# A graph layer with edge groups of 1024 instead of 512, and its linear attention moved into the edge loop

## The chip, the cores and the metric

One core of a Trainium2 chip. The metric is the device time of one execution in microseconds (us). A profiled execution has a span of its own, from its first to its last recorded instruction; the execution's device time is a little longer. The engines are PE (TensorE, matrix products), DVE (VectorE), ACT (ScalarE), POOL (GpSimd) and SP (SyncE, which here only issues DMAs).

## The reference

The input is `x`, 3125 nodes of 256 features, and 50,000 edges sorted by their target node. In short:

```python
xn = layernorm(x)                                   # without scale and shift
h  = einsum('ni,hio->hno', xn, W)                   # 4 heads of 64
e  = leaky(attn_src[:, src] + attn_dst[:, dst], 0.2) * edge_weight
e_exp = exp(e - max(e))                             # one maximum over all edges and heads
alpha = e_exp / (segment_sum(e_exp, dst)[dst] + 1e-10)
gnn = segment_sum(h[:, src] * alpha, dst)
q, k, v = split(xn @ W_qkv)                         # 4 heads of 32
k = softmax(k over the nodes); context = k^T v; mix = (context, q * 32**-0.5) @ W_out + b_out
x1 = x + gnn + mix
n2 = layernorm(x1); weights = n2 @ wr + br
y  = (gelu(n2 @ w1 + b1) @ w2 + b2) * weights       # for the 1561 nodes of highest weight, else 0
out = x1 + y + n2
```

All products are in fp32. The division by the sum of the exponentials is made once per node at the end, so the edge work only accumulates `h[src] * e_exp` and `e_exp` per target node.

## The kernel before, in words

Nodes are held in 25 blocks of 128 (`NB`), in groups of `BODY` = 5. `x`, the accumulator `acc` (260 columns: 256 features and 4 denominators) and most else stay in SBUF. The kernel has three stages.

**First stage.** DVE normalises a block (`normed`, L742), PE turns it (two transposes, L429), ACT copies it to `xnT` (L603). PE's `project` then multiplies it with a weight of 392 columns (L414: `h`, the two attention terms of the edges, and `v`; two contraction halves, and each fp32 product is recorded as two passes, so 4 passes) and makes `k` and `q` (L420, 8 passes of 128 columns), which ACT copies out (L592). DVE's `evacuate_h` copies the 260 columns `h` and `attn_src` to `hst` (L749) and the other 132 to `adv` (L750). SP stores each block's `hst` to the table `htab` in DRAM (`store_rows`, L282). Between those stores SP also issues the loads of late weights and, from block 15 to 22, the index lists of edge groups 0 to 7 (`step`, L293 to L300, five DMAs per group). POOL adds `b_out` to `x` block by block (L362).

**Edge stage.** Edges are taken in groups of `TILES` x 128 = 512, 98 groups. For each, POOL issues 4 indirect DMAs, each gathering 128 rows of `htab` by source node into `G` (L380). `G` has `RING` = 4 groups, the lists `LISTS` = 8. POOL waits for the list and, from group 4 on, until DVE has read the old group out of the slot (`messages_ready`). The work per group g:

- DVE builds `ohT`, the edges' columns of one target block (L855); PE's `expand` multiplies it with `attn_dst` (L449, 12 small products); DVE adds the gathered `attn_src` (L896), takes the leaky part and the edge weight (L900, L904) and the maximum (L908, `rm`).
- PE's `turn` lays the 128 maxima along a row (L470), DVE's `group_max` (L915) makes the running maximum, ACT takes the exponentials (L656 into `msg`, L657 into PSUM), DVE multiplies the gathered rows with them (`messages`, L921) and builds the one-hot matrix `oh` of the targets within their block (L983).
- PE's `sums` multiplies `oh` with `msg` (L474, 4 tiles, 8 passes of 260 columns), and DVE's `add_last` adds the result to `acc` of the block, scaled by the change of the maximum (L926). ACT computes that scale (`rescale`, L633, L636). A group that lies across two node blocks (24 of the groups) has its sums split by ACT with two masks (`split_sums`, L646) and added twice by DVE.

`et`, `msg`, `oh` and the PSUM banks of `sums` exist twice. DVE makes the logits of group g+2 and the columns of g+3 while group g is summed, and adds the sums of g-1 during step g. On every engine the edge loop is written by `groups` (L204): 8 steps unrolled, a hardware loop of 11 turns with 8 steps each, and 10 steps unrolled.

**Linear attention.** It stands between the preparation of the first edge groups and the edge loop: ACT exponentiates `k` (L611); PE turns each block of it (L508) and sums `v` against it (L512); the context is multiplied by `W_out` into `C2` (L517, L1015); PE multiplies each block's `q` by `C2` (L522, 2 passes of 256 columns) and DVE adds it to `x` (L1019). Only then DVE and PE enter the edge loop.

**Tail.** DVE divides and adds (L1062, L1066), normalises again, PE runs the two products of the feed-forward part (L552, L565), DVE ranks the weights by counting (L1111, L1114), POOL weights the result, SP stores it.

Each engine runs its own program in order; the order is written out by hand, and semaphores join the engines.

Of the kernel before, what the change touches and what calls it, by code (L numbers as in the profile page):

```python
# [19 lines left out]
TILES = 4  # L20
RING = 4
LISTS = 8
BODY = 5


def gps_layer(nc, x_in, src_in, dst_in, ew_in, gw_in, gas_in, gad_in, wqkv_in, wout_in, bout_in,
# [25 lines left out]
    ADV = HEADS + QK  # L52
    HW = ROW + ADV
# [8 lines left out]
    LOOPS = NG // LISTS  # L62
    KSEL = max(1, int(0.5 * N))
    KK = KSEL - 1 if KSEL > 1 else 1
    assert EREST % TILES == 0 and D == HF == 256 and NB % BODY == 0 and QK == P

    htab = nc.dram_tensor("htab", (NB * P, ROW), F32, kind="Internal").ap()
    dstu_d = nc.dram_tensor("dstu_d", (NG, GE), U16, kind="Internal").ap()
    dstm_d = nc.dram_tensor("dstm_d", (NG * GE,), I32, kind="Internal").ap()
    meta_d = nc.dram_tensor("meta_d", (NG, 3), I32, kind="Internal").ap()  # L70
    low_d = nc.dram_tensor("low_d", (NG, 1), I32, kind="Internal").ap()
    w_d = nc.dram_tensor("w_d", (NB, P), F32, kind="Internal").ap()

    with ExitStack() as ctx:
# [10 lines left out]
        kq = sb("kq", [P, 2, NB * P])  # L85
        adv = sb("adv", [P, NB, ADV])
        wbig = sb("wbig", [P, KC, HW])
        wqk = sb("wqk", [P, KC, 2 * QK])
# [8 lines left out]
        boutb = sb("boutb", [P, D])  # L97
# [7 lines left out]
        xnT = sb("xnT", [P, BODY, KC, P])  # L105
# [15 lines left out]
        meta = sb("meta", [1, NG * 3], I32)  # L121
        neg1 = sb("neg1", [1, PAD], I32)
# [5 lines left out]
        dmr = sb("dmr", [P, LISTS, TILES], I32)  # L128
# [10 lines left out]
        et = sb("et", [P, 2, 17])  # L139
        rm = sb("rm", [P, 2])  # L140
# [9 lines left out]
        kmaxs = sb("kmaxs", [P, NB // BODY])  # L150
        ekt = sb("ekt", [P, BODY, P])
# [6 lines left out]
        dm = wide[0:NG, 0:GE].bitcast(I32)  # L158
# [6 lines left out]
        wrow = kq[:, 0, :]  # L165
        junk = kq[:, 1, :]
# [6 lines left out]
        for name in ("constants_ready y_weighted gelu_table masks_ready k_padding_zero wqkv_loaded "  # L173
                     "block_iota_ready kmax_of_batch sp_go gp_go dve_go act_go deviation_ready b_out_loaded "
                     "w_loaded late_weights_loaded a_loaded w_times_a w_a_ready stats_ready mean_var_ready "
                     "rstd_ready xn_ready xn_turned xnT_ready h_projected rows_staged attn_dst_v_taken "
                     "kq_projected kq_taken b_out_added dst_loaded table_steps tables_stored ranges_loaded "
                     "last_dst_loaded padding_loaded attn_dst_split kmax_steps k_exp ksum_steps ek_turned "
                     "ek_taken context_summed context_taken c2_multiplied c2_taken mix_multiplied mix_added "
# [17 lines left out]
        FIRST_BATCHES = ((0, 1), (1, BODY - 1))  # L197
        TURN_BANKS, MIX_BANKS = (3, 4, 6), (3, 4, 6)
        WT_AT = 6
        DLP = 12  # L200

        block = ctx.enter_context(nc.Block())

# [947 lines left out]
```

## Time and profile before

| | us |
|---|---|
| three executions | 818.95, 821.65, 824.38 |
| median | 821.65 |
| profiled execution, device time | 820.17 |
| its span | 818.0 |
| busy: PE, DVE, POOL, ACT | 666.8, 593.3, 467.2, 224.4 |
| mean granted TensorE clock (1 is full speed) | 0.849 |

The busy time of PE counts modelled ends of pipelined products. The shares over the whole span mix the three stages, so the stages have to be read one by one. The page also lists where the chain of work that ended last went: PE 28%, issue 21%, DVE 17%, POOL 14%, DMA 11% ("issue" is time in which an engine waited for nothing that the profile shows).

### The profile page before, as it was taken

Reading aid. Unit: us, or ns where it says so; the run is one execution under the profiler, and the core shown is the slowest. Engines: PE = TensorE matmul, PEld = TensorE weight load, DVE = VectorE, ACT = ScalarE, POOL = GpSimd, SP = SyncE. Lnnn points to the kernel's source line nnn. Section 1 sums busy time; section 2 is a strip of 40 time slices with the busy share of each in tenths; the row PEclk is TensorE's granted clock in tenths of the full one; section 3 lists DMA queues with packets and bytes.
Section 4 is the critical chain, followed back from the end, with each engine's and each line's share of the span. In section 5 each row is a group of like instructions: output and inputs, shape, how many; then the busy total and the mean of one; then the engine's idle time right before and its main releaser. Section 6 shows DMA issues by size and latency. Waiting matters only on the chain.

```text
span 818.0 us, 18313 instructions
## 1 busy us (share of the span) xinstructions
PE 666.8 (82%) x4271; PEld 548.8 (67%) x4272; DVE 593.3 (73%) x1631; ACT 224.4 (27%) x817; POOL 467.2 (57%) x512
## 2 busy tenths in 40 slices
PE   3799687776878786878886878788859989999995
PEld 2577575554656564756675666666648879999994
DVE  7566268666767685867686868687789973989895
ACT  1132512111222122213232323232333423323331
POOL 5134246777777777777777777777721350333332
PEclk9899888887787678778677978686888989999998
DMA  7264325655556565656555555566410001000000
GB/s 212 58 181 75 87 72 114 138 138 136 134 135 143 131 139 134 140 133 138 137 135 134 139 135 138 132 138 140 108 35 1 1 12 71 33 26 27 27 27 22
DMA packets 104859, 82.97 MB, mean 101 GB/s; under 512 B 67133, under 2 KB 91566, under 8 KB 104561
## 3 DMA queue, kind: packets, MB, share of 16 engines
q0 software_dynamic: 18816, 52.21, 24.9%
q1 hardware_dynamic: 85873, 29.16, 16.8%
q14 instruction: 145, 1.19, 0.5%
q8 instruction: 25, 0.41, 0.2%
HBM read 74.47 MB, written 6.84 MB: 99 GB/s over the span
## 4 chain that ended last, share of the span: by engine, by line
PE 28%; issue 21%; DVE 17%; POOL 14%; DMA 11%; DVEq 5%; SPq 2%; ACT 1%; ACTq 0%; POOLq 0%
POOL G L380 13%; DMA G<-htab,srcr 9%; PE ps L552 8%; PE ps L565 8%; PE ps L414 4%; PE ps L474 4%; DVE msg L921 3%; PE ps L420 2%; DVEq L228 2%; DVE wprod L1079 1%; DMA x<-in_x 1%; DVE oh L983 1%; DVE G L1062 1%; DVE x L1066 1%; DVE x L1019 1%
## 5 line engine op out<-in xcount | busy, mean ns | idle before, releaser
L380 POOL DMA_INDIRECT G<-htab,srcr x392 | 372.9, 951 | 150.7 <-issue 127.7
L474 PE MATMUL ps<-msg,oh 128*128 128x260 f32 x784 | 265.9, 498 | 78.4 <-DVE oh L983 76.8
L474 PEld LDWEIGHTS ps<-msg,oh 128*128 128x128 f32 x784 | 183.0, 245 | 116.2 <-issue 83.3
L921 DVE TENSOR_TENSOR msg<-G,ps 128x1024 f32<-128x1024 f32 x98 | 118.7, 1212 | 29.1 <-issue 28.1
L552 PEld LDWEIGHTS ps<-xnT,w 128*128 128x128 f32 x800 | 98.3, 201 | 3.8 <-issue 1.8
L552 PE MATMUL ps<-xnT,w 128*128 128x128 f32 x800 | 98.8, 285 | 2.1 <-ACT wide L712 1.6
L656 ACT ACTIVATE msg<-et,negR 128x16 f32<-128x16 f32 x98 | 30.1, 308 | 224.2 <-DVE rj L915 178.7
L565 PE MATMUL ps<-w,wide 128*128 128x256 f32 x400 | 90.4, 380 | 1.0 <-DVE acc L1086 1.0
L565 PEld LDWEIGHTS ps<-w,wide 128*128 128x128 f32 x400 | 74.3, 190 | 10.2 <-issue 1.3
L393 POOL TENSOR_SCALAR G<-acc,mw 128x256 f32<-128x256 f32 x25 | 23.1, 923 | 99.6 <-DVE mw L1119 90.4
L983 DVE TENSOR_TENSOR oh<-ps,dmr 128x512 f32<-128x512 f32 x98 | 67.2, 686 | 17.0 <-issue 16.8
L449 PE MATMUL ps<-ad,ohT 128*128 x1464 | 77.3, 176 | 2.4 <-DVE ohT L855 1.3
L470 PEld LDWEIGHTS ps<-ident,rm 128*128 128x128 f32 x196 | 43.2, 243 | 49.9 <-DVE rm L908 43.1
L449 PEld LDWEIGHTS ps<-ad,ohT 128*128 128x128 bf16 x1464 | 67.3, 118 | 8.5 <-issue 2.5
L470 PE MATMUL ps<-ident,rm 128*128 128x128 f32 x196 | 51.4, 352 | 22.4 <-DVE rm L908 22.2
L712 ACT ACTIVATE wide<-ps,b 128x128 f32<-128x128 f32 x200 | 54.3, 390 | 3.5 <-PE ps L552 3.4
L386 POOL TENSOR_TENSOR x<-x,acc 128x256 f32<-128x256 f32 x25 | 22.0, 885 | 48.7 <-DVE acc L1072 48.7
L1114 DVE TENSOR_SCALAR_CACHE_REDUCE kq<-kq,wtok 128x3125 f32<-128x3125 f32 (+24 forms) x25 | 46.6, 1865 | 0.0
L633 ACT ACTIVATE fsc<-negRlast,negR 128x1 f32 x98 | 28.8, 294 | 61.4 <-issue 30.1
L1111 DVE TENSOR_SCALAR_CACHE_REDUCE kq<-kq,wtok 128x128 f32<-128x128 f32 (+23 forms) x24 | 44.9, 1871 | 0.0
L414 PE MATMUL ps<-wbig,xnT 128*128 128x392 f32 x100 | 40.5, 531 | 4.9 <-DVE adv L750 4.7
L855 DVE TENSOR_SCALAR ohT<-dstb,nodeid 128x512 bf16<-128x512 uint16 x98 | 38.0, 387 | 8.5 <-issue 7.2
(135 smaller groups left out, 722.5 us busy)
## 6 DMA issues: line engine op xcount, KB each, us to landing
dstb<-dstu_d SPq DMA_DIRECT2D x98, 128.0 KB
G<-htab,srcr POOLq DMA_INDIRECT x392
htab<-hst SPq DMA_DIRECT2D x25, 130.0 KB, 2.8
out<-G SPq DMA_DIRECT2D x24, 128.0 KB, 1.7
x<-in_x SPq DMA_DIRECT2D x4, 640.0 KB, 8.0
w<-in_L_ffn_w SPq DMA_DIRECT2D x4, 512.0 KB
kq<-w_d SPq DMA_DIRECT2D x1, 1600.0 KB, 6.4
dmr<-dstm_d SPq DMA_DIRECT2D x98, 2.0 KB
```

The lines of the kernel that those rows point to most:

```text
L380: gp.indirect_dma_start(G[:, q % RING, k, :], None, htab, bass.IndirectOffsetOnAxis(ap=srcr[:, q, k:k + 1], axis=0)).then_inc(s_g[q % RING ...
L414: m = pe.matmul(ps[:, 2 + b, 0:HW], xnT[:, t % BODY, kc, :], wbig[:, kc, :], start=(kc == 0), stop=(kc == KC - 1))
L449: m = pe.matmul(ps[:, p, 4 * k:4 * k + 4], ohT[:, columns, k:GE:TILES], ad3[:, bass.ds(b, 1), j, :].rearrange("p a h -> p (a h)"), start=F ...
L470: pe.matmul(ps[:, 2, 0:P], rm[:, q % 2:q % 2 + 1].to_broadcast([P, P]), ident[:, :], start=True, stop=True).then_inc(S["max_turned"], 1)
L474: m = pe.matmul(ps[:, 3 + p, 0:ROW], oh[:, p, k, :], msg[:, p, k, :], start=(k == 0), stop=(k == TILES - 1))
L552: m = pe.matmul(ps[:, 2 + half, (c % 4) * P:(c % 4 + 1) * P], w1[:, kc, c * P:(c + 1) * P], xnT[:, t % BODY, kc, :], start=(kc == 0), stop ...
L565: m = pe.matmul(ps[:, 4 + t % 3, 0:D], hT[:, t % 2, c, :], w2[:, c, :], start=(c == 0), stop=(c == FC - 1))
L712: m = act.activation(hT[:, t % 2, c, :], ps[:, 2 + half, (c % 4) * P:(c % 4 + 1) * P], ACT.Gelu_apprx_tanh, bias=b1[:, c:c + 1])
L921: dve.tensor_tensor(msg[:, p, :, 0:HF].rearrange("p k (h o) -> p k h o", h=HEADS), G[:, q % RING, :, 0:HF].rearrange("p k (h o) -> p k h o ...
L983: dve.tensor_tensor(oh[:, q % 2, :, :], iotap.unsqueeze(1).to_broadcast([P, TILES, P]), dmr[:, q, :].unsqueeze(2).to_broadcast([P, TILES, ...
L1111: dve.tensor_scalar(junk[:, 0:lo], wrow[:, 0:lo], wt, 0.0, ALU.is_ge, ALU.add, accum_out=cnt[:, t, 0:1]).then_inc(S["counted"], 1)
L1114: dve.tensor_scalar(junk[:, lo:N], wrow[:, lo:N], wt, 0.0, ALU.is_gt, ALU.add, accum_out=cnt[:, t, 1:2]).then_inc(S["counted"], 1)
```

## The change

- **First stage.** `wbig` has 264 columns (`h` and both attention terms), so `project` is 4 passes of 264 columns and nothing else. `xnT` keeps all 25 blocks. `evacuate_h` moves from DVE to ACT (260 columns to `hst`, 4 to `adst`). `k` is projected after the last block, in 7 chunks of 512 nodes (`keys`), which DVE takes together with their maximum. The tables of the edges (`table_steps`) lose two steps on DVE and one cast moves to ACT. `b_out` is no longer added to `x` by POOL, which zeroes `acc` block by block instead. Blocks 1 to 9 of `x` are loaded by ACT's queue. Of the lists SP issues only that of group 0 before the last stores (at block 19); the other three and the late weights come behind them.
- **Edge stage.** Groups of 1024 (`TILES` = 8), 49 of them, `RING` = 2, `LISTS` = 4, four list DMAs per group. Messages, one-hot matrices and sums go in two halves of 4 tiles; POOL waits for the first half of the messages before the first 4 gathers and for the second half before the other 4. `et`, `rm`, `msg`, `oh` and the bank of `sums` exist once. DVE makes the logits of group g+1 in step g, all four operations in a row, and adds the sums of g at the end of step g itself. `dmod`, the target within its block, is masked by DVE instead of loaded. PE's program is written out for all 49 groups; the other engines loop over turns of 4 groups.
- **Linear attention.** It runs inside the loop: during groups 3 to 22 PE makes `v` of one block and the turned `k` (`make_pair`), ACT copies both out (`take_pairs`); at group 23 the context is closed and multiplied into `M` = (W_q x `C2`), so that the second half multiplies `xnT` itself by `M` (`mix`, with `b_out` as a first product with a row of ones, 6 passes of 256 columns) and DVE adds the result to `x` (`add_mix`). One block per group, two in every fourth (`BLOCKS`).
- **Tail.** Unchanged.

The core of the diff ("-" before, "+" after):

```diff
-TILES = 4
-RING = 4
-LISTS = 8
+TILES = 8
+HALF = 4
+RING = 2
+LISTS = 4
+BLOCKS = ((0,), (1,), (2,), (3, 4))
...
-        xnT = sb("xnT", [P, BODY, KC, P])
+        xnT = sb("xnT", [P, NB, KC, P])
-        msg = sb("msg", [P, 2, TILES, ROW])
-        oh = sb("oh", [P, 2, TILES, P])
+        msg = sb("msg", [P, TILES, ROW])
+        oh = sb("oh", [P, TILES, P])
...
# SP
                 for t in range(NB):
                     store_rows(t)
-                    if 2 <= t < 2 + len(loads):
-                        sp.dma_start(loads[t - 2][0], loads[t - 2][1])...
-                    if NB - LISTS - 2 <= t < NB - 2:
-                        step(t - (NB - LISTS - 2), t - (NB - LISTS - 2))
-                groups(step, peeled=False)(sp)
+                    if t == TABLES_AT:            # 9
+                        store_tables()
+                    if t == TABLES_AT + 6:
+                        spread_tables()
+                    if t in LISTS_AT:             # (19,)
+                        step(LISTS_AT.index(t), LISTS_AT.index(t))
+                unrolled(step, range(len(LISTS_AT), LISTS))
+                for tile, array in loads:
+                    sp.dma_start(tile, array).then_inc(S["late_weights_loaded"], 16)
+                looped(sp, 1, LOOPS - 1, step)
+                unrolled(step, TAIL)
...
# POOL
+                for k in range(TILES):
+                    if k % HALF == 0 and (g is None or g >= RING):
+                        gp.wait_ge(S["messages_ready" if k else "messages_half"], n)
+                        gp.sem_inc(S["gp_go"], 1)
+                    gp.indirect_dma_start(G[:, q % RING, k, :], None, htab, ...)
...
# PE
+            def sums(g):
+                ...
+                pe.wait_ge(S["added_last"], g + 1)
+                pe.wait_ge(S["messages_half"], g + 1)
+                pe.wait_ge(S["onehot_half"], g + 1)
+                add_messages(range(HALF))
+                pe.wait_ge(S["messages_ready"], g + 1)
+                pe.wait_ge(S["onehot_last"], g + 1)
+                add_messages(range(HALF, TILES)).then_inc(S["summed_last"], 1)
+            def mix(t):
+                bank = 4 + t % BODY % 2
+                if t:
+                    pe.wait_ge(S["mix_added"], t + 1 if t % BODY in (0, 1, 2, 3) else t)
+                pe.matmul(ps[:, bank, 0:D], ones[:, :], bout[:, :], start=True, stop=False)
+                for kc in range(KC):
+                    m = pe.matmul(ps[:, bank, 0:D], xnT[:, t, kc, :], M[:, kc, :], start=False, stop=(kc == KC - 1))
+                m.then_inc(S["mix_multiplied"], 1)
+            for g in range(NG):
+                sums(g)
+                if g + 1 < NG:
+                    turn(g + 1)
+                if g + 2 < NG:
+                    if g % 2 == 0:
+                        load_ranges(pe, regs, cursor, (g + 2) % LISTS)
+                    expand(g + 2)
+                if MADE_AT <= g < MADE_AT + TURNS * LISTS:      # 3 to 22
+                    ... make_pair(i * BODY + s)
+                if g == MIXED_AT:                               # 23
+                    multiply_context()
+                if MIXED_AT <= g < MIXED_AT + TURNS * LISTS:    # 23 to 42
+                    ... mix(i * BODY + s)
...
# ACT
+            def evacuate_h(t):
+                act.wait_ge(S["h_projected"], t + 1)
+                if t >= BODY:
+                    act.wait_ge(s_tab[t % BODY], 16 * (t // BODY))
+                act.activation(hst[:, t % BODY, :], ps[:, 2 + t % 2, 0:ROW], ACT.Copy)...
+                act.activation(adst[:, t, :], ps[:, 2 + t % 2, ROW:HW], ACT.Copy)...
...
+                rescale(fsc, p, last, "factor_last", n, "max_kept_last")
+                if side:
+                    side(q)
+                split_sums(q)
...
# DVE
+            def step(g, q, side=None):
+                dve.wait_ge(S["exp_ready"], n)
+                visit(g, q)            # messages, one-hot, messages, one-hot
+                if g is None or g + 1 < NG:
+                    if g is None or g + 1 < NG - 1:
+                        mask_dst((q + 1) % LISTS)
+                    logits((q + 1) % LISTS, n1, g if g is None else g + 1)
                 if g is None or g + 2 < NG:
+                    if q % 2 == 0:
+                        load_ranges(dve, regs, cursor, (q + 2) % LISTS)
+                    columns((q + 2) % LISTS)
+                if g is None or g + 1 < NG:
+                    group_max(q + 1, n1)
+                if side:
+                    side(q)
+                add_last(q)
...
-            groups(step)(dve)
+            unrolled(step, FIRST)
+            looped(dve, 1, 1 + TURNS, step)
+            take_context()
+            looped(dve, 1 + TURNS, LOOPS - 1, step, add_mix)
+            unrolled(step, TAIL)
```

## Rows read from the trace of the kernel before

**Rows 1.** Windows by stage: length; PE, PEld, DVE, ACT, POOL busy; clock, DMA share, GB/s.

```profile
126.00:300.00 174.00, 137.75 (x849) 106.03 (x847) 121.65 (x359) 38.00 (x155) 131.83 (x139) 0.79 0.61 136
...
608.50:818.00 209.50, 187.94 (x1251) 176.22 (x1251) 170.18 (x407) 67.71 (x234) 63.29 (x75) 0.95 0.07 24
```

**Rows 2.** Groups of instructions, by line: busy us, mean ns, idle before and its releasers.

```profile
L380 POOL DMA_INDIRECT G<-htab,srcr x392 | 372.9, 951 | 150.7 <-issue 127.7 <-DVE msg L921 23.0
L474 PE MATMUL ps<-msg,oh 128*128 128x260 f32 x784 | 265.9, 498 | 78.4 <-DVE oh L983 76.8 <-issue 1.4
```

**Rows 3.** Timeline of POOL: start us, us, engine, line, operation, [idle before <-releaser].

```profile
94.40 1.16 POOL L380 DMA_INDIRECT G<-htab,srcr  x1 [20.41 <-issue]
...
125.73 0.94 POOL L380 DMA_INDIRECT G<-htab,srcr  x1 [11.43 <-DVE msg L921]
...
306.46 0.95 POOL L380 DMA_INDIRECT G<-htab,srcr  x1 [0.30 <-DVE msg L921]
...
596.56 0.95 POOL L380 DMA_INDIRECT G<-htab,srcr  x1 [0.30 <-issue]
```

**Rows 4.** Timeline of the first stage.

```profile
26.06 0.40 DVE L742 TENSOR_SCALAR xn<-x,mv,rstd 128x256 f32<-128x256 f32 x1
...
77.78 0.38 PE L429 MATMUL ps<-ident,xn 128*128 128x128 f32 x2
78.00 1.48 PE L414 MATMUL ps<-wbig,xnT 128*128 128x392 f32 x4
...
80.43 1.48 PE L414 MATMUL ps<-wbig,xnT 128*128 128x392 f32 x4
...
84.16 0.43 DVE L749 COPY hst<-ps 128x260 f32<-128x260 f32 x1 [1.58 <-PE ps L414]
...
90.52 0.82 SPq L282 DMA_DIRECT2D htab<-hst  x2
```

**Rows 5.** Chain that ended last: start us, us, what.

```profile
90.91 2.27 DMA htab<-hst
```

**Rows 6.** Groups by line: copies on ACT and the attention's add on DVE.

```profile
L636 ACT ACTIVATE negRlast<-negR 128x1 f32 x122 | 24.8, 203 | 14.4
L603 ACT ACTIVATE xnT<-ps 128x256 f32<-128x256 f32 x25 | 9.4, 376 | 2.2 <-PE ps L429 2.2
L1019 DVE TENSOR_TENSOR x<-ps,x 128x256 f32<-128x256 f32 x25 | 10.6, 425 | 2.6 <-PE ps L522 2.4
```

**Rows 7.** Timeline of the last groups.

```profile
598.34 0.57 PE L449 MATMUL ps<-ad,ohT 128*128 x12
...
599.57 0.17 DVE L896 TENSOR_TENSOR et<-ps,G 128x16 f32<-128x16 f32 x1
...
600.94 0.49 PE L470 MATMUL ps<-ident,rm 128*128 128x128 f32 x2 [0.17 <-DVE rm L908]
...
602.71 0.34 DVE L915 TENSOR_SCALAR_CACHE_REDUCE rj<-ps,negR 128x128 f32<-128x128 f32 x1
...
603.60 1.22 DVE L921 TENSOR_TENSOR msg<-G,ps 128x1024 f32<-128x1024 f32 x1
604.74 0.68 DVE L983 TENSOR_TENSOR oh<-ps,dmr 128x512 f32<-128x512 f32 x1
605.16 0.88 ACT L646 ACTIVATE hst<-ps,mask 128x260 f32<-128x260 f32 x2 [1.59 <-PE ps L474]
...
605.57 1.99 PE L474 MATMUL ps<-msg,oh 128*128 128x260 f32 x8 [0.63 <-DVE oh L983]
...
606.99 0.49 DVE L926 SCALAR_TENSOR_TENSOR acc<-acc,fsc,hst 128x260 f32 x1 [0.24 <-DVE acc L926]
...
608.03 0.48 DVE L926 SCALAR_TENSOR_TENSOR acc<-acc,fsc,ps 128x260 f32 x1 [0.55 <-PE ps L474]
```

**Rows 8.** Timeline at a loop jump.

```profile
322.54 1.22 DVE L921 TENSOR_TENSOR msg<-G,ps 128x1024 f32<-128x1024 f32 x1 [3.19 <-issue]
...
324.50 3.81 PE L474 MATMUL ps<-msg,oh 128*128 128x260 f32 x8 [3.80 <-DVE oh L983]
```

More of the change, by code:

```diff
@@ L72, in gps_layer @@
     w_d = nc.dram_tensor("w_d", (NB, P), F32, kind="Internal").ap()
+    NORMED = ((0, 1), (1, BODY - 1)) + tuple((lo, BODY) for lo in range(BODY, NB, BODY))
     with ExitStack() as ctx:
@@ new lines, in sums @@
+                pe.wait_ge(S["messages_half"], g + 1)
[4 more added lines that the diff above has]
+                add_messages(range(HALF, TILES)).then_inc(S["summed_last"], 1)
+            load_ranges(pe, regs, cursor, 0)
+            expand(0)
+            expand(1)
+            for c in range(2, CHUNKS):
+                keys(c)
+            pe.wait_ge(S["k_taken"], CHUNKS)
@@ new lines, in _, with add_context @@
+            for kc in range(KC):
+                m = pe.transpose(ps[:, 5, kc * P:(kc + 1) * P], wqkv[:, kc, 0:QK], ident[:, :])
+            m.then_inc(S["query_turned"], 1)
+            pe.matmul(ps[:, 6, 0:P], zrow[:, 0:P], zrow[:, 0:P], start=True, stop=False, skip_group_check=True)
+            turn(0)
+            def add_context(t):
+                pe.wait_ge(S["pair_taken"], t + 2)
+                return pe.matmul(ps[:, 6, 0:P], pair[:, t % BODY, 0:P], pair[:, t % BODY, P:2 * P], start=False, stop=(t == NB - 1), skip_group_check=True)
@@ new lines, in make_pair @@
+            def make_pair(t):
+                bank = 4 + t % BODY % 2
+                if t == 0:
+                    pe.wait_ge(S["query_taken"], 1)
+                    pe.wait_ge(S["k_padding_zero"], 1)
+                pe.wait_ge(S["k_exp"], 1 + t // BODY)
+                if t:
+                    pe.wait_ge(S["pair_taken"], t + 1 if t % BODY in (0, 1, 2, 3) else t)
+                for kc in range(KC):
+                    pe.matmul(ps[:, bank, 0:P], xnT[:, t, kc, :], wqkv[:, kc, 2 * QK:3 * QK], start=(kc == 0), stop=(kc == KC - 1))
+                pe.transpose(ps[:, bank, P:2 * P], kT[:, t * P:(t + 1) * P], ident[:, :]).then_inc(S["pair_made"], 1)
+                if t >= 2:
+                    add_context(t - 2)
@@ new lines, in _ @@
+            load_ranges(dve, regs, cursor, 0)
+            columns(0)
+            dve.wait_ge(S["attn_dst_last"], 1)
+            columns(1)
+            for c in range(CHUNKS):
+                lo, hi = c * WIDE, min((c + 1) * WIDE, N)
+                dve.wait_ge(S["k_projected"], c + 1)
+                dve.tensor_scalar(kT[:, lo:hi], ps[:, 5 + c % 2, 0:hi - lo], 1.0, LOWEST, ALU.mult, ALU.max, accum_out=kmaxs[:, c:c + 1]).then_inc(S["k_taken"], 1)
+            dve.memset(kT[:, N:NB * P], 0.0).then_inc(S["k_padding_zero"], 1)
@@ new lines, in add_mix @@
+            def add_mix(q):
+                for s in BLOCKS[q]:
+                    t = dve.snap(u, min_val=0, max_val=NB - 1)
+                    a = x[:, bass.ds(t, 1), :].rearrange("p a c -> p (a c)")
+                    dve.wait_ge(S["mix_multiplied"], mixed)
+                    dve.sem_inc(S["dve_go"], 1)
+                    dve.tensor_tensor(a, ps[:, 4 + s % 2, 0:D], a, ALU.add).then_inc(S["mix_added"], 1)
+                    dve.reg_add(u, u, 1)
+                    dve.reg_add(mixed, mixed, 1)
```

669 lines of the change are left out of this document (293 added, 376 removed).

## The prediction

> **What bounds the kernel now.** I read the windows by stage first [rows 1]. The edge stage runs at a mean granted clock of .79 of the full level, with POOL at 131.8 of 174 us and neither PE nor DVE full; the tail takes 209.5 us and the diff does not touch it. Next, the groups of instructions: 392 gathers of .951 us each, and almost all of POOL's idle time before them is "issue" [rows 2]. POOL's timeline then gives the skeleton of the run [rows 3]: the first gather starts at 94.40, one stall of 11.43 us stands at 125.73 (DVE and PE are in the linear attention and do not free the ring), the last gather ends at 597.51. (597.51 - 94.40 - 11.13) / 392 = 1.255 us per gather, and a gather with its usual gap is .95 + .30 = 1.25. So POOL issues without pause, and everything else keeps up. The span is first gather 94.4 + gathers 492.0 + stall 11.1 + drain to the last add 11.0 (608.51 - 597.51) [rows 3, 7] + tail 209.5 = 818.0; the profiled execution took 820.17, so 2.2 us lie around the span. It stands .2% under the median 821.65.
>
> Two further things bear on the change. The first gather waits for the table's last store, issued from 90.52 although its rows were staged at 84.16: SP was issuing lists in between [rows 4]. It lands 2.27 us after 90.91 [rows 5], and POOL starts 1.2 us later. And the loop is not as smooth as POOL shows it: at a jump DVE loses 3.19 us of "issue" and the sums after it run in 3.81 us instead of 1.99 [rows 7, 8], the two levels of the clock (1.2 and 2.4 GHz). The ring of four groups absorbs this; POOL's own jump costs it .30, no more than any gap [rows 3].
>
> **First stage: a certain gain.** A block now costs 2.43 us (78.00 to 80.43) [rows 4]. PE keeps .22 for the turning (77.78 to 78.00) and 4 passes of 264 columns; the sums' passes of 260 columns take 1.99 / 8 = .25 each [rows 7], so 1.0, and with an estimated .06 between them 1.28 us per block. ACT beside it copies xnT .38, 260 columns .44 (half of .88) and 4 columns .20 [rows 6, 7]: 1.02, hidden, but only .26 short of becoming the bound. DVE no longer evacuates, so block 5, the first that waits for PE, is normalised about 1.7 us before its 26.06 [rows 4], at 24.4. Twenty blocks at 1.28 are 25.6; I add 2.5 for a start at half clock (two blocks twice as long) and 1.2 for the last block's turning: 53.7. Then .45 for the copy, .39 to the issued store (90.52 to 90.91), 2.27 and 1.2: **first gather at 58.0**, bounds 54 (no slow start, block 0 earlier) and 63 (1.5 us per block). SP issues one list before the last stores and 12 list DMAs behind them, .41 each [rows 4], 5 us, before the second group's gathers end. The 25 small memsets that replace the 25 adds on POOL lie before its first gather, beside the projections.
>
> **Gathers: unchanged.** 392 x 1.255 = 492.0. The fifth list DMA per group and the attention's own stall (11.1) go; what keeps POOL waiting now is counted as X below.
>
> **The loop: what is paid for the gain.** POOL needs 8 x 1.255 = 10.04 us per group of 1024. With single buffers the rest becomes one serial chain per group, read off the last groups [rows 7]: messages to sums 1.97 (603.60 to 605.57), the sums s, about .1, turn .49, about .05, maximum to messages .89 (602.71 to 603.60): 3.5 + s. The expansion (24 products, 2 x .57) and the logits lie beside the sums. For 16 passes s is 3.98 at the full level, 7.62 at half [rows 7, 8], and by the mean of all groups 2 x 265.9 / 98 = 5.43 [rows 2]. The chain is then 7.5, 11.1, or 8.9: under POOL's 10.04 by 1.1 on the mean, over it at half clock, and the ring now holds two groups. I take the mean, since the work per edge on PE is nearly the same, and keep the other two as ends.
>
> What comes on top in the second half: add_mix .43 [rows 6] before add_last, which itself moves into the chain: .48 after the sums, less cover, +.35 in an ordinary group; in one that lies across two blocks the split .88 and the second add .73 (.24 + .49) [rows 7], +1.1; I take .88, as 14 of the groups 24 to 43 are such. Two blocks fall into every fourth group, +.43. DVE's jump, now every four groups, costs about 2.9 (3.19 less its .30), and the sums behind it run at half clock, +2.2 against the mean. Four groups: 4 x (8.93 + .88) + .43 + 2.9 + 2.2 = 44.8 against POOL's 40.2: 4.6 lost, five times, 23. In the first half the pair's passes lie in PE's gaps and the split comes less often: 4 x 9.4 + 2.9 = 40.5 with no dip, some .6 lost, five times, 3. Start-up: the second group's successor waits for the exponentials of the keys in front of group 0's; between 0 and the 11.4 of before's stall [rows 3] I take 2, because only seven chunks and five exponentials are left there. Closing the context at group 23 is a serial chain of about ten short steps over DVE, PE and ACT at .4 to .5 each [rows 6, 7]: 5, bounds 2 and 8. The last groups all lie across blocks: 7. **X = 40**, ends 9 (chain always 7.5 + extras, under POOL) and about 72 (mean s between mean and half clock). Unrolling PE in itself I cost at nothing: at the jump PE waits for DVE's one-hot, not for itself [rows 8].
>
> **Drain.** From the last gather to the first logits 2.06 (597.51 to 599.57), to the turn's end 1.9, then maximum to messages 1.2, messages to sums 2.0, 16 passes 4.0 to 7.6, split and two adds 2.1 [rows 7]: 13 to 17 with POOL last, up to 19.5 if the chain runs behind POOL, as I expect there; I take 17.5.
>
> **Sum:** 58.0 + 492.0 + 40 + 17.5 + 209.5 = 817.0, plus 2.2 around it: **819 us**, 1 less than the profiled run, .3% under the median. Break-even is X = 42.
>
> At this point the Trainium skill speaks against the change: "Double-buffer for performance: Overlap DMA with compute" (Trainium Kernel Development and Optimization, Best Practices), where the change halves each buffer's number. By it alone rival B would be the forecast; the mean chain of 8.9 under 10.04 says that one buffer still suffices between jumps.
>
> **Rivals.** *A, the clock stays up.* If the passes of the attention keep PE at the full level in the loop, s = 3.98, the chain 7.5 to 8.8 absorbs the jumps, X = 9, drain 14: 58 + 492 + 9 + 14 + 209.5 + 2.2 = 785. For: PE's work is spread evenly; the tail, dense, shows .95 [rows 1]. Against: .79 in the loop with the attention outside it, and a chain with more serial waits than before. *B, the serial chain (slower).* If s is 6.5, midway between mean and half, the chain is 10.0 and always lags: first half 4 x 10.5 + 2.9 = 44.9, 4.7 lost five times; second half 4 x 10.88 + .43 + 2.9 = 46.9, 6.7 lost five times; with 2 + 5 + 8 for the rest X = 72, drain 19.5: **853**. For: every wait in the chain lets PE idle, and the sums after an idle stretch are the slow ones [rows 8]. Against: the mean of before includes such waits. It decides from X = 51 on. *C, the jump gets cheaper.* DVE's loop body has four steps instead of eight, and POOL's short body shows no jump cost at all [rows 3]. Then the jump costs .30 and its dip goes: X = 14, 793. The Trainium skill has a rule that could make this so (Runtime: NRT & Kernel Launch, Instruction fetch mechanics): a taken branch to a target outside the resident instructions waits for a fetch. Against: four steps of 1024 in halves hold nearly as many instructions as six of the old. *D, the first stage does not do what it promises:* ACT and its waits for the stores pace it, 2.0 per block, first gather at 72: 833.
>
> **How the numbers follow.** Forecast (X from 27 to 54: 806 to 834) .46; A .22 (776 to 794); B .18 (840 to 866); C .08; D .06. A change of 1% is 8.2 us: about what can be told from no change here. Faster (under 813.4): A, C and .12 of the forecast's range, .42. Slower (over 829.9): B, .07 of the forecast and .05 of D, .30. The rest, .28, lies within 1%. Cases of both signs hold most of it; the likeliest one's own range is 806 to 834. The range 778 to 858 takes in most of A and B and leaves out about .1 of each side's tails together.
>
> **What will show it.** First gather at 58 (54 to 63): later means ACT or the late lists, seen as what ends PE's idle time before the projection. POOL's idle time "<-DVE msg", 23.0 before, should grow to about 40 and sit mostly at the jumps of the second half; none there is A or C (told apart by the sums' mean, 5.4 against 4.0 per 16 passes, and by DVE's "issue" at the jump), in every group is B. The granted clock in the loop near .79. From the last gather to the last add 17.5. The tail 209.5; another length would make the forecast wrong by a mechanism that I have not seen.

## The result

The changed kernel takes 813.41 us (median of 11 executions, 810.47 to 815.19) against 819.48 us before (median of 11, 816.63 to 824.38): ratio .9917, 95% interval .99 to .9934. That is .8% faster, inside the band of 1% that the prediction called no change, and 5.6 us under the 819 that it gave. The profiled execution took 810.47 with a span of 808.7, so it is the lowest of the eleven; a stage read from it is a few us better than the median.

### The profile page after: what moved, and what is told of

The parts are those of the page before. It is cut to its first block, busy times and chain, and to the rows that moved or that the text cites. A ratio compares the mean times of both kernels' runs of the same rounds, so it can differ in the third digit from the quotient of the medians.

```text
span 808.7 us, 15213 instructions
## 1 busy us (share of the span) xinstructions
PE 700.1 (87%) x4447; PEld 594.0 (73%) x4448; DVE 518.4 (64%) x1246; ACT 185.9 (23%) x651; POOL 452.5 (56%) x511
## 4 chain that ended last, share of the span: by engine, by line
PE 50%; POOL 15%; issue 14%; DVE 14%; DMA 4%; DVEq 2%; ACT 1%; ACTq 0%; POOLq 0%; SPq 0%
PE ps L489 15%; POOL G L387 14%; PE ps L600 8%; PE ps L613 8%; PE ps L465 7%; PE ps L561 3%; DMA G<-htab,srcr 3%; PE ps L424 2%; PE ps L559 2%; DVE wprod L1110 1%; DVE stats L794 1%; DVE G L1093 1%; PE ps L437 1%; DVE x L1097 1%; DVE msg L937 1%
## 5 line engine op out<-in xcount | busy, mean ns | idle before, releaser
L387 POOL DMA_INDIRECT G<-htab,srcr x392 | 373.9, 954 | 162.0 <-issue 124.6
L489 PE MATMUL ps<-msg,oh 128*128 128x260 f32 x784 | 246.3, 483 | 28.8 <-DVE oh L951 28.6
L465 PE MATMUL ps<-ad,ohT 128*128 x1752 | 116.5, 201 | 13.1 <-DVE ohT L908 9.4
L465 PEld LDWEIGHTS ps<-ad,ohT 128*128 128x128 bf16 x1752 | 112.3, 167 | 16.0 <-issue 15.0
L951 DVE TENSOR_TENSOR oh<-ps,dmod 128x512 f32<-128x512 f32 x96 | 65.5, 682 | 0.0
L699 ACT ACTIVATE hst<-ps,mask 128x260 f32<-128x260 f32 x48 | 20.3, 473 | 169.8 <-PE ps L489 169.8
L932 DVE TENSOR_SCALAR_CACHE_REDUCE rj<-ps,negR 128x128 f32<-128x128 f32 x48 | 16.7, 348 | 47.5 <-PE ps L485 45.1
L1145 DVE TENSOR_SCALAR_CACHE_REDUCE xnT<-kT,wtok 128x3125 f32<-128x3125 f32 (+24 forms) x25 | 46.6, 1865 | 0.0
L1142 DVE TENSOR_SCALAR_CACHE_REDUCE xnT<-kT,wtok 128x128 f32<-128x128 f32 (+23 forms) x24 | 44.9, 1870 | 0.0
L908 DVE TENSOR_SCALAR ohT<-dstb,nodeid 128x1024 bf16<-128x1024 uint16 x49 | 24.3, 496 | 31.4 <-issue 28.8
L561 PE MATMUL ps<-M,xnT 128*128 128x256 f32 x100 | 37.3, 508 | 0.0
```

The lines of the kernel that those rows point to most:

```text
L387: gp.indirect_dma_start(G[:, q % RING, k, :], None, htab, bass.IndirectOffsetOnAxis(ap=srcr[:, q, k:k + 1], axis=0)).then_inc(s_g[q % RING ...
L465: m = pe.matmul(ps[:, p, 4 * k:4 * k + 4], ohT[:, columns, k:GE:TILES], ad3[:, bass.ds(b, 1), j, :].rearrange("p a h -> p (a h)"), start=F ...
L489: m = pe.matmul(ps[:, 3, 0:ROW], oh[:, k, :], msg[:, k, :], start=(k == 0), stop=(k == TILES - 1))
L561: m = pe.matmul(ps[:, bank, 0:D], xnT[:, t, kc, :], M[:, kc, :], start=False, stop=(kc == KC - 1))
L908: dve.tensor_scalar(ohT[:, 0, :], dstb[:, q, :], nodeid[:, bass.ds(last, 1)], None, ALU.is_equal).then_inc(S["columns_last"], 1)
L951: return dve.tensor_tensor(oh[:, tiles, :], iotap.unsqueeze(1).to_broadcast([P, HALF, P]), d.unsqueeze(2).to_broadcast([P, HALF, P]), ALU. ...
```

## The profile after, beside the one before

The windows by stage of the changed kernel, the columns as in [rows 1]:

```profile
110.00:207.00 97.00, 80.79 (x512) 68.49 (x511) 56.04 (x128) 14.68 (x52) 71.77 (x77) 0.83 0.52 135
...
318.00:450.00 132.00, 126.44 (x780) 101.04 (x778) 77.37 (x185) 21.89 (x79) 89.68 (x95) 0.81 0.47 121
...
583.00:599.00 16.00, 11.82 (x35) 9.07 (x34) 6.94 (x14) 2.34 (x8) 0.00 (x0) 0.68 0.03 8
599.00:808.70 209.70, 187.39 (x1252) 175.52 (x1251) 171.12 (x408) 69.08 (x238) 63.25 (x75) 0.94 0.07 24
```

The first number after the length is PE's busy time. In the first half of the loop it is 80.8 of 97 us; in the second half 126.4 of 132, that is 96%, where the kernel before had 137.8 of 174 (79%) [rows 1]. The clock is no lower than before (.83 and .81 against .79). So PE has become full, which the prediction had looked for nowhere.

The groups of instructions (busy us, mean ns, idle before and its releasers):

```profile
L387 POOL DMA_INDIRECT G<-htab,srcr x392 | 373.9, 954 | 162.0 <-issue 124.6 <-DVE msg L937 37.4
L489 PE MATMUL ps<-msg,oh 128*128 128x260 f32 x784 | 246.3, 483 | 28.8 <-DVE oh L951 28.6
L465 PE MATMUL ps<-ad,ohT 128*128 x1752 | 116.5, 201 | 13.1 <-DVE ohT L908 9.4 <-DVE ohT L905 3.7
L561 PE MATMUL ps<-M,xnT 128*128 128x256 f32 x100 | 37.3, 508 | 0.0
L559 PE MATMUL ps<-bout,ones 1*128 1x256 f32 x50 | 20.8, 499 | 0.7 <-ACT M L744 0.7
```

The sums take 246.3 / 49 = 5.03 us per group of 1024 (5.43 by the rows of before), and PE waits for VectorE's one-hot only 28.6 us in all against 76.8 [rows 2]. New are 58 us of mix (L561, L559).

POOL's timeline, which answers to [rows 3]; the rows with a wait of over 2 us before them, and the first and the last gather:

```profile
57.78 1.16 POOL L387 DMA_INDIRECT G<-htab,srcr  x1 [10.70 <-issue]
...
82.94 0.94 POOL L387 DMA_INDIRECT G<-htab,srcr  x1 [5.27 <-DVE msg L937]
...
206.53 0.96 POOL L387 DMA_INDIRECT G<-htab,srcr  x1 [2.38 <-issue]
...
332.44 0.94 POOL L387 DMA_INDIRECT G<-htab,srcr  x1 [6.86 <-DVE msg L937]
...
356.04 0.94 POOL L387 DMA_INDIRECT G<-htab,srcr  x1 [2.35 <-issue]
...
420.32 0.94 POOL L387 DMA_INDIRECT G<-htab,srcr  x1 [4.57 <-DVE msg L937]
...
505.75 0.94 POOL L387 DMA_INDIRECT G<-htab,srcr  x1 [4.54 <-DVE msg L937]
...
508.93 0.94 POOL L387 DMA_INDIRECT G<-htab,srcr  x1 [2.23 <-issue]
...
551.09 0.94 POOL L387 DMA_INDIRECT G<-htab,srcr  x1 [3.51 <-DVE msg L937]
...
582.03 0.95 POOL L387 DMA_INDIRECT G<-htab,srcr  x1 [0.30 <-issue]
```

These rows give the balance, with the numbers of before from [rows 3, 7]. The first gather is 36.6 us earlier (94.40 to 57.78) and the attention's stall of 11.1 is gone: 47.7 gained. Given back: POOL waits 32.1 us between the gathers (each wait of over .45 less its usual .30), 1.1 in smaller ones, and the drain from the last gather to the last add grew from 11.0 to 18.4 (582.98 to 601.39). The tail is 2.2 shorter. -47.7 + 32.1 + 1.1 + 7.4 - 2.2 = -9.3, the difference of the spans (818.0 - 808.7).

The 32.1 us by place: 5.0 at group 2, 6.6 at group 26 (the closing of the context), 9.9 in the groups 30 to 42, of them 4.3 at group 34 and 4.2 at group 42, 4.6 in the groups 46 to 48, and 6.1 in three pauses of POOL that name no releaser ("issue", groups 14, 28 and 42). POOL's group 34 goes into the slot of group 32 and waits for the messages of that group. What lies behind this wait is seen in PE's and VectorE's timeline some groups earlier, where group 31 ends and VectorE's loop jumps to group 32:

```profile
401.83 2.97 PE L465 MATMUL ps<-ad,ohT 128*128 x47
404.74 0.69 PE L559 MATMUL ps<-bout,ones 1*128 1x256 f32 x2
405.36 1.13 PE L561 MATMUL ps<-M,xnT 128*128 128x256 f32 x4
406.42 1.12 PE L559 MATMUL ps<-bout,ones 1*128 1x256 f32 x2
407.47 2.08 PE L561 MATMUL ps<-M,xnT 128*128 128x256 f32 x4
409.34 5.67 PE L489 MATMUL ps<-msg,oh 128*128 128x260 f32 x16
414.85 0.39 PE L485 MATMUL ps<-ident,rm 128*128 128x128 f32 x2
...
408.23 0.19 DVE L926 TENSOR_REDUCE rm<-et 128x1 f32<-128x32 f32 x1
...
415.27 0.35 DVE L932 TENSOR_SCALAR_CACHE_REDUCE rj<-ps,negR 128x128 f32<-128x128 f32 x1 [5.89 <-PE ps L485]
...
418.31 1.22 DVE L937 TENSOR_TENSOR msg<-G,ps 128x1024 f32<-128x1024 f32 x1 [0.23 <-issue]
```

PE has no gap at all here: the expansion of a group that lies across two blocks (2.97), two blocks of mix (404.74 to 409.34, the second at half clock), then the sums. The maximum of the next group was ready at 408.42 and is turned at 414.85, because the sums stand before it. VectorE waits 5.89 us for it. And the jump itself, at 418.31, costs .23 us of "issue", where before it cost 3.19 [rows 8].

## Experiments

Ratios are to the kernel before, measured beside each run; the changed kernel has .9917, from the runs of the section on the result. A profile shows one execution, and the one shown can lie some us off the median. Theory P was formed from the rows above: PE's own work is the bound of the second half, and the wait falls where two blocks of mix stand between two sums. Its rival J is the prediction's term (VectorE's jump and a serial chain of single buffers). Theory S concerns the start: the first gather is not what counts there.

### VectorE's loop written out

```diff
-            looped(dve, 1, 1 + TURNS, step)
+            for g in range(TURNS * LISTS):
+                step(None, g % LISTS)
             take_context()
-            looped(dve, 1 + TURNS, LOOPS - 1, step, add_mix)
+            for g in range(TURNS * LISTS):
+                step(None, g % LISTS, add_mix)
```

> The changed kernel with VectorE's two loops of the edge stage written out (40 steps, the same instructions in the same order), so that VectorE never jumps between groups. Theory P (TensorE's own work is the bound of the second half: 126.4 us busy of 132 us between 318 and 450 in the changed kernel, and the waits of GpSimd lie where two blocks' products stand between two sums): no change, 813 +- 3 us, and the waits of 4.3 to 4.6 us at the groups 34 and 42 stay. Rival J (the prediction's term: VectorE's jump costs about 2.9 us every four groups and the sums behind it run at half clock): the waits at 34 and 42 go, 10 to 20 us less, 793 to 803 us.

Measured: 814.63 us, ratio .9919 (.9893 to .9945), no change. POOL's timeline has the same waits:

```profile
423.51 0.94 POOL L387 DMA_INDIRECT G<-htab,srcr  x1 [3.99 <-DVE msg L937]
...
508.88 0.94 POOL L387 DMA_INDIRECT G<-htab,srcr  x1 [4.17 <-DVE msg L937]
```

The jump costs nothing; J's price for it is refuted.

### b_out added by GpSimd

```diff
+                gp.tensor_tensor(x[:, t, :], x[:, t, :], boutb[:, :], ALU.add)...
...
-                pe.matmul(ps[:, bank, 0:D], ones[:, :], bout[:, :], start=True, stop=False)
```

> The changed kernel without the product of a row of ones and b_out in each block's mix (4 passes instead of 6); GpSimd adds b_out to x in the first stage, as the kernel before did, where it is idle. Theory P: a third of the mix leaves TensorE (20.8 us busy in all); between the groups 24 and 48 GpSimd waits 14 us outside its own 2 us pauses, of which about 9 hang on the mix; 5 to 9 us less, 804 to 808 us. Rival J: VectorE's order and jumps are the same, within 2 us of 813.

Measured: 803.04 us, ratio .9765 (.9733 to .9797), 1.5% or 12 us less than the changed kernel; more than expected. POOL's waits in the groups 27 to 45 (without its own pauses) fall from 9.9 to .5, those of the last three from 4.6 to 3.7, all waits from 32.1 to 24.8. The two profiled executions differ by 6.3 us (804.15 against 810.47), less than the medians, because the changed kernel's is its best one and this one lies 1 us over its median. PE is now at 117 of 132 us:

```profile
318.00:450.00 132.00, 117.35 (x764) 97.27 (x763) 80.36 (x191) 22.27 (x80) 92.17 (x98) 0.81 0.47 124
```

A third of the mix off PE is enough to free POOL in the groups 27 to 45. P holds.

### One block of the mix per group

```diff
-                if MIXED_AT <= g < MIXED_AT + TURNS * LISTS:
-                    i, s = divmod(g - MIXED_AT, LISTS)
-                    for s in BLOCKS[s]:
-                        mix(i * BODY + s)
+                if MIXED_AT <= g < MIXED_AT + NB:
+                    mix(g - MIXED_AT)
```

(and VectorE's adds alike, in its last five steps too)

> The changed kernel with the 25 blocks of the mix spread over the groups 24 to 48, one each, instead of over 24 to 43 with two in every fourth. Same products and adds in all. Theory P: the waits of 4.3 us at group 34 and 4.2 at group 42 shrink to under 1 each, the last five groups get one mix each more (about 2.5 us of TensorE at half clock, of which they have little to spare: up to 5 us given back); 2 to 8 us less, 805 to 811 us. Rival J: nothing moves at the jumps, the waits at 34 and 42 stay, 813 or a few us more.

Measured: 799.66 us, ratio .9745 (.9712 to .9777), 1.7% or 14 us less; more than expected, and the five later blocks cost nothing: the waits of the last three groups went from 4.6 to 1.6. At the two places POOL's rows are now:

```profile
418.62 0.95 POOL L387 DMA_INDIRECT G<-htab,srcr  x1 [0.76 <-DVE msg L935]
...
501.02 0.95 POOL L387 DMA_INDIRECT G<-htab,srcr  x1 [0.74 <-DVE msg L935]
```

The same work, laid otherwise, takes 14 us less with PE nearly as full in this stretch (124.6 of 132), so how the load lies is what hurt, more than its sum. The edit changes two things in that: no group has two blocks any more, and a fifth of the mix moves out of the groups 24 to 43 into the last five. The two are not told apart. The size of the ring is no part of it: `G` holds 16 tiles of 128 rows in both kernels (4 x 4 and 2 x 8), and the kernel before carried the 3.2 us of a jump with them [rows 8].

### The keys' exponentials behind the first groups

```diff
-            for i in range(NB // BODY):
-                exponentiate(i)
...
+            for g in FIRST:
+                step(g, g)
+                exponentiate(g)
+            exponentiate(LISTS)
```

> The changed kernel with the five exponentials of the keys on ScalarE moved from before the first group's exponentials to behind the steps of groups 0 to 3. Theory S (the 5.0 us wait of GpSimd at group 2 is set by the chain keys, exponentials of the keys, exponentials of group 0, messages, and not by the gathers): the wait goes and nothing later takes it back, 4 to 5 us less, 808 to 809 us. Rival G (given back): the second half, where TensorE is full, starts earlier but ends no earlier, 812 to 814 us.

Measured: 810.99 us, ratio .9873 (.9848 to .9898), .4% or 4 us less (the intervals just do not meet). That lies between S and G. The wait at group 2 is halved, not gone: 2.67 at 81.33 instead of 5.27. What is left is the keys' own products, the first half of them at half clock (granted .50 from 63.5 to 69), and a table load of 1.28 us that now stands in front of the first group's exponentials. The rows of the changed kernel show the whole chain:

```profile
63.51 10.04 PE L437 MATMUL ps<-xnT,wqkv 128*128 128x512 f32 x20
...
74.96 1.28 ACT L674 ACT_TABLE_LOAD   x1
76.26 0.83 ACT L674 ACTIVATE kT<-kT,kmax 128x640 f32<-128x640 f32 x1
...
80.27 0.30 ACT L716 ACTIVATE msg<-et,negR 128x32 f32<-128x32 f32 x1
```

### The expansion in one product of 12 columns

```diff
-                    for j in range(3):
-                        m = pe.matmul(ps[:, p, 4 * k:4 * k + 4], ..., ad3[:, bass.ds(b, 1), j, :]...)
+                    m = pe.matmul(ps[:, p, 12 * k:12 * k + 12], ..., ad3[:, bass.ds(b, 1), :, :]...)
...
+                dve.tensor_reduce(ekh, ps[...].rearrange("p (k j h) -> p k h j", ...), AX.X, ALU.add)...
```

> The changed kernel with the three parts of attn_dst in one product of 12 columns instead of three of 4 (584 products in the expansion instead of 1752), VectorE sums the three parts in one more operation of about .25 us per group. Theory P: TensorE's expansion falls from 116.5 us to about 40 and its load below GpSimd's 10.04 us per group; the waits at the groups 34, 42 and 46 to 48 shrink to a few tenths, the drain after the last gather by about 1; 8 to 13 us less than the changed kernel, ratio to the kernel before .976 to .982. Rival C (clock): with less work TensorE is granted the half level for longer, and the operation on VectorE lengthens the chain; ratio .988 to 1.00.

Measured: 800.02 us, ratio .977 (.9741 to .9798), 1.5% less: P, with its number. The three parts were three loads of the same one-hot weights. The mean of one product is the same with three times the columns, and since the products overlap, PE is busy 75 ns per product (43.9 / 584) where it was 66 (116.5 / 1752):

```profile
L464 PE MATMUL ps<-ad,ohT 128*128 x584 | 43.9, 206 | 15.1 <-DVE ohT L907 9.2 <-DVE ohT L904 5.9
```

The waits of the last three groups are gone, the drain is 16.8 instead of 18.4. The wait at group 42 stays at 3.6: the two blocks in the fourth group are still there. The clock between 318 and 450 stays at .81, against rival C.

### The kernel before, with its lists late

```diff
-                    if NB - LISTS - 2 <= t < NB - 2:
-                        step(t - (NB - LISTS - 2), t - (NB - LISTS - 2))
+                    if t == 15:
+                        step(0, 0)
+                for q in range(1, LISTS):
+                    step(q, q)
```

> The kernel before with one thing of the changed one: the index lists of the groups 1 to 7 are issued behind the table's last stores instead of between them (group 0's at block 15). The first gather should start near 88.5 instead of 94.4. Theory S (the start of the gathers is not the start that counts: group 2's ring slot, or in this kernel the linear attention's end, sets when GpSimd goes on): the wait of 11.43 us at 125.7 grows by what the start gains, no change, 820 +- 2. Rival G (the prediction counted this as 6 us of the gain): 5 to 6 us less.

Measured: 816.35 us, ratio .9961 (.9946 to .9976), 3 us less. The rows:

```profile
86.41 1.16 POOL L382 DMA_INDIRECT G<-htab,srcr  x1 [13.80 <-issue]
...
120.55 0.94 POOL L382 DMA_INDIRECT G<-htab,srcr  x1 [14.11 <-DVE msg L923]
```

The start is 8.0 earlier, the wait 2.7 longer. Neither S (nothing) nor G (5 to 6) is right: the stall is set by the attention's end, as S says, but that end came 5.2 us earlier too (125.73 to 120.55). The trace of the kernel before shows what waited. VectorE takes the first groups' logits before it goes on with the attention, and there it waited for the gathered rows, 6.66 us and 2.84 us; with the early gathers its first such wait is .93 (at 94.13).

```profile
101.17 0.17 DVE L896 TENSOR_TENSOR et<-ps,G 128x16 f32<-128x16 f32 x1 [6.66 <-DMA G<-htab,srcr]
...
106.18 0.17 DVE L896 TENSOR_TENSOR et<-ps,G 128x16 f32<-128x16 f32 x1 [2.84 <-DMA G<-htab,srcr]
```

### All four lists before the last store

```diff
-        TABLES_AT, LISTS_AT = 9, (19,)
+        TABLES_AT, LISTS_AT = 9, (20, 21, 22, 23)
```

> The changed kernel with all four first lists issued by SP before the table's last store (at the blocks 20 to 23) instead of one. The first gather should start about 4 us later, near 62. Theory S (the wait of 5.3 us at group 2 is set by the keys' chain, so the first gather has as much to spare): the wait at group 2 shrinks by what the start loses, same time within 2 us. Rival G (the start counts in full, as the prediction summed it): 4 us more, ratio .996 to .998.

Measured: 817.35 us, ratio .9963 (.9945 to .998), .5% or 4 us more than the changed kernel. The first gather is not 4 but 8.2 us later, at 66.01, and the wait at group 2 is gone:

```profile
66.01 1.16 POOL L387 DMA_INDIRECT G<-htab,srcr  x1 [18.25 <-issue]
```

So the wait at group 2 is set by the keys, as S says, and the time still rises, as G says. By the medians, 8.2 later less 5.0 absorbed leaves 3.2, near the 4 measured. The traces do not show this sum: POOL's waits from group 26 on (without its own pauses) are 24.7 instead of 21.0, and its last gather ends 8.0 later (590.96 against 582.98), so most of what was saved at group 2 is waited again later. The changed kernel's trace is its fastest execution and this one is near its median. How much later the first gather may start for nothing stays open.

### GpSimd's loop written out

```diff
-            looped(gp, 1, LOOPS - 1, step)
+            for g in range((LOOPS - 2) * LISTS):
+                step(None, g % LISTS)
```

> The changed kernel with GpSimd's loop of the edge stage written out. GpSimd pauses 2 to 4 us with no releaser at the second gather of the groups 14, 28 and 42 in every profile of the changed kernel and its variants, 112 gathers apart, and nowhere in the kernel before. If its instruction stream is the cause (fetch at the loop), the three pauses go or move; if it is something that counts gathers (a ring of descriptors), they stay at the same gathers. Time in the first case up to 6 us less, in the second the same within 2 us.

Measured: 812.49 us, ratio .9922 (.9893 to .9951), no change, and the three pauses stand at the same gathers:

```profile
207.81 0.95 POOL L387 DMA_INDIRECT G<-htab,srcr  x1 [3.62 <-issue]
...
355.74 0.94 POOL L387 DMA_INDIRECT G<-htab,srcr  x1 [2.36 <-issue]
...
508.65 0.94 POOL L387 DMA_INDIRECT G<-htab,srcr  x1 [2.23 <-issue]
```

So POOL's loop is not the cause: the pauses go with the number of the gather. That number alone isn't the cause either, for the kernel before makes the same 392 gathers without a pause. What it is stays open.

### Without the mix

The second half of the attention is left out, products and adds.

```diff
-                if MIXED_AT <= g < MIXED_AT + TURNS * LISTS:
-                    ...
-                        mix(i * BODY + s)
...
-            looped(dve, 1 + TURNS, LOOPS - 1, step, add_mix)
+            looped(dve, 1 + TURNS, LOOPS - 1, step)
```

> The changed kernel without the second half of the attention: the products of mix and their adds are left out (x gets neither context nor b_out); all else stays. Theory P: the waits at the groups 30 to 42 go; those at 26, 46 to 48 and the three pauses stay, about 21 of 32 us: 9 to 14 us less than the changed kernel, ratio .975 to .981, no better than e3, which keeps the whole work. Rival (the chain of single buffers itself lags): some 4 us less, ratio .987.

Measured: 799.40 us, ratio .9756 (.9729 to .9784), as P expected, and no better than the even mix (.9745), which does all the work. POOL's waits add up to the 21 us of the expectation, but not at its places: those of the last three groups are gone too, and 2.8 are left in the groups 27 to 45. One thing was not expected, in the windows of this kernel:

```profile
318.00:450.00 132.00, 107.57 (x698) 88.85 (x698) 75.59 (x179) 22.10 (x79) 91.92 (x97) 0.76 0.47 124
```

With 18.9 us less work on PE the granted clock is .76 instead of .81, and the sums take 260.8 us instead of 246.3. So part of what the mix costs PE, it gives back to the sums. This is the one run that shows it: with a third of the mix away, or with the expansion merged, the clock of the same stretch stays at .81, and with all four edits it is .83, though PE has less work there in each of them (117.4, 111.9 and 95.9 us).

### Three and four of the edits together, and an earlier first group

> The edits of e2, e3 and e4 together, with the three products per tile kept. Theory P: with one mix of 4 passes per group TensorE stays just under GpSimd in the second half, but the drain and the last groups keep the long expansions: 3 to 6 us behind the kernel with all four, ratio .965 to .973. Rival: the expansion is what counts, ratio .974 or more.

Measured: 796.71 us, ratio .9734 (.9695 to .9774), at the edge of the range given, with an interval that takes in P's range and its rival's, so it decides nothing between them. It is no different by its interval from the even mix alone: the three edits share one slack.

> The edits of e2, e3, e4 and e5 together in the changed kernel. By theory P and S the waits left to GpSimd are about 3 at group 2, 4 to 5 at the closing of the context and its own three pauses (9): 58 to 59 + 492 + 16 to 18 + a drain of 14 + 207.3 + 2 = 789 to 792, ratio .960 to .968. If the four share one and the same slack (rival), no better than the best of them alone, .974 to .977.

Measured: 794.40 us, ratio .9699 (.9672 to .9726), a little outside .960 to .968. By its median it is better than any edit alone, though its interval touches that of the even mix (.9712 to .9777). It is 3% under the kernel before and 2.2% under the changed one (.9699 / .9917). In the profiled execution (789.69, the fastest of its seven) POOL's gathers run from 58.08 to 565.11, 15 us over their 492, of which 6 are its own pauses; PE has room again:

```profile
318.00:450.00 132.00, 95.93 (x450) 73.37 (x451) 84.46 (x202) 24.32 (x85) 96.15 (x101) 0.83 0.48 127
```

The wait for the context is 1.9 instead of 6.6.

The last one adds to these four:

```diff
             for c in range(2, 5):
                 keys(c)
+            turn(0)
+            for c in range(5, CHUNKS):
+                keys(c)
```

(VectorE takes the first group's logits and maximum between the chunks 4 and 5, ScalarE copies W_q behind the first group)

> All four edits, and the first group's logits, maximum and exponentials taken before the last two chunks of the keys and before W_q is copied. Theory S: the wait at group 2 (about 3 us) goes, 2 to 3 us less than with the four alone, ratio .957 to .965. Rival G: given back at the closing of the context, no change.

Measured: 796.85 us, ratio .9731 (.9704 to .9758), no gain. VectorE came to the logits before the gathered rows and stood:

```profile
74.03 0.19 DVE L923 TENSOR_TENSOR et<-et,G 128x32 f32<-128x32 f32 x1 [1.76 <-DMA G<-htab,srcr]
```

So the last two chunks went behind it, and the first messages started at 80.00 instead of 77.37. In an in-order queue an early place is an early wait.

## Why the prediction was right and wrong

- **First gather at 58.0**: 57.78. The two parts of the sum were both off and cancelled: a block takes 1.11 us (49.43 to 50.54 in the rows below), not 1.28, since its four passes take .89 (49.43 to 50.32) instead of 1.0 and nothing lies between blocks; but the projections go on later (the fifth block's at 26.39, after 2.27 us of waiting for ScalarE's copy) and wait once more, 1.50 us, behind a copy that waited for a store (the last two rows). What the sum missed is that 5.0 of the 36.6 us gained are waited off again at group 2: its slot hangs on the keys, not on the gathers. The wait is gone when the gathers start later, and halved when the keys' exponentials move.

```profile
49.43 1.06 PE L424 MATMUL ps<-wbig,xnT 128*128 128x264 f32 x4
50.32 0.38 PE L445 MATMUL ps<-ident,xn 128*128 128x128 f32 x2
50.54 1.06 PE L424 MATMUL ps<-wbig,xnT 128*128 128x264 f32 x4
...
44.10 0.39 ACT L647 ACTIVATE hst<-ps 128x260 f32<-128x260 f32 x1 [2.39 <-DMA htab<-hst]
44.88 1.16 PE L424 MATMUL ps<-wbig,xnT 128*128 128x264 f32 x4 [1.50 <-ACT xnT L662]
```

- **Gathers 492.0**: 492 and 1.1 in small gaps, plus 6.1 us of pauses that no row of before could show.
- **X = 40**: 33.2, by other terms than the prediction's. Start-up 2: 5.0. First half 3: none outside a pause. Context 5: 6.6. Second half 23: 9.9. Last groups 7: 4.6. (The 3 of the first half was itself mis-added: 40.5 less 40.2 is .3 in four groups, not .6.)
- **The step that failed** is "DVE's jump, now every four groups, costs about 2.9 ... and the sums behind it run at half clock, +2.2". The jump costs .23, and writing the loop out moves nothing. Rival C had this right, though not its time, since PE's load took the place of the jump: a body of four steps behaves like POOL's short one. Without these two terms the second half's 23 would have been 0 (44.8 - 5.1 is under 40.2). In the kernel before all nine jumps of VectorE's loop (ten turns, not eleven: 8 + 80 + 10 = 98 groups) cost 2.7 to 3.5 us; in the changed one they cost at most .24. The profile's queue of instruction loads (`q14`; packets, MB, share) goes the same way, and between 160 and 320 us it has 45 packets in the kernel before and none in the changed one:

```profile
q14 instruction: 145, 1.19, 0.5%
...
q14 instruction: 25, 0.20, 0.1%
```

The first row is the kernel before, the second the changed one. The loops of eight steps load their code anew in every turn, those of four steps do not; which engine's code a packet holds, the row does not say. The Trainium skill's rule beside C (Runtime: NRT & Kernel Launch, Instruction fetch mechanics), that a branch out of the resident instructions waits for a fetch, agrees with these rows and with 3.19 and .23.

- **The step that was missing** is PE's own load. The sum priced the mix by VectorE's add alone (.43) and took its passes at nothing, as it put the pair's into PE's gaps; the expansion was put beside the sums. On PE nothing lies beside the sums: it is one queue. Between 318 and 450 lie twelve groups and the closing of the context (4 us of products): (126.4 - 4) / 12 = 10.2 us of PE's work per group against POOL's 10.04, and in a fourth group the second block's mix adds 2.9 (406.42 to 409.34). Taking a third of the mix off PE, spreading it, or merging the expansion each removes or shrinks the waits (merging leaves 3.6 at group 42). Two blocks stand in the steps 26, 30, 34, 38 and 42; POOL pays for them four groups later at 34, 42 and 46, but .4 or less at 30 and 38, right after longer waits. Why those two cost next to nothing was not looked into.
- **A (clock stays up)**: the sums' mean is 5.03, a little better than the 5.4 taken; the clock .81 to .83. Not the case. **B (chain always behind)**: the waits are not in every group; refuted. **D**: refuted by 57.78.
- **Drain 17.5**: 18.4. The last 16 passes run between the two levels of the clock (granted .60): 6.25 us, where 3.98 is the full level and 7.62 half.

```profile
592.63 6.25 PE L489 MATMUL ps<-msg,oh 128*128 128x260 f32 x16 [4.18 <-DVE oh L951]
```

- **Tail 209.5**: 207.3, in every variant of the changed kernel 206.4 to 207.3; its cause was not looked for.

The time came out near because the missing load and the pauses (9.9 + 6.1) stood where the jump had been put (23). That was luck; that the sum agreed is not evidence for its terms. The rule of the Trainium skill that was weighed (Trainium Kernel Development and Optimization, Best Practices: double-buffer) speaks of overlapping DMA with compute, and the buffer of the gathers, `G`, is still double here. No run gives `msg`, `oh` or the sums a second buffer, so what the single ones cost is not measured; with them the four edits bring POOL to within 15 us of its 492.

## What to carry to other kernels

When work moves into a loop "beside" the bound engine, add it up per turn on each engine's own queue, at the mean of the clock seen there, and compare it with the bound's turn; a gap in an average is not a gap where two pieces fall together. Where the bound engine can run ahead by only two groups, spread an uneven load over the turns. Where a loop jump costs, see whether the profile's instruction queue moves in every turn. Before an early start is counted as a gain, look for the next thing that the started engine waits for.

## What the runs showed of the hardware that was not expected

- POOL pauses 2 to 4 us at the second gather of the groups 14, 28 and 42, 112 gathers apart, in all profiles of the changed kernel and its variants, and in none of the kernel before and its variant; it does not depend on POOL's loop.
- A product with 128 x 128 weights of its own takes the same .20 us with 12 columns as with 4 (206 and 201 ns); overlapped, 75 and 66 ns of PE's busy time each.
- Taking the whole mix off PE lowered its clock from .81 to .76 in the same stretch, and the remaining sums took 6% longer. Three other edits that took work off PE left the clock at .81 or .83.
- VectorE's hardware loop of eight steps lost 2.7 to 3.5 us at each jump while instruction loads ran in every turn (45 packets in 160 us); the loop of four steps lost at most .24 us, with no such load in the same 160 us.
